# Attention 2's closing: half of the output projection moved ahead of the last score units, and its bias as one bf16 product

## The reference, cut to what matters

```python
def _L1_xattn_ref(x, cond, Wq, bq, Wkv, bkv, Wp, bp):
    ...
    q = _fq_sym(q, axis=-1)
    k = _fq_sym(k, axis=-1)
    v = _fq_sym(v, axis=2)
    attn = jnp.einsum('bhqd,bhkd->bhqk', q, k)
    attn = jax.nn.softmax(attn.astype(jnp.float32), axis=-1)
    attn = _fq_unsigned(attn, axis=-1)
    out = jnp.einsum('bhqk,bhkd->bhqd', attn, v)
    out = jnp.transpose(out, (0, 2, 1, 3)).reshape(B, N, C)
    return out @ Wp + bp
```

## Time and profile before

| what | value |
|---|---|
| time, median of 3 executions | 891.05 us (890.66 to 892.91) |
| the profiled execution's own time | 892.17 us |
| its span, first to last instruction | 890.4 us |
| PE busy | 714.0 us (80%) |
| DVE busy | 534.0 us (60%) |
| ACT busy | 368.7 us (41%) |
| POOL busy | 303.3 us (34%) |
| mean granted TensorE clock | 0.889 |

### The profile page before, as it was taken

The page is one execution under the profiler, slowest core; times in us unless marked ns, Lnnn a source line. Parts: engine busy times, 40 slices in busy tenths (PEclk is TensorE's granted clock), DMA queues, the critical chain, the costliest instruction groups (busy, mean ns, idle before and its releaser), DMA issues.

```text
span 890.4 us, 14503 instructions
## 1 busy us (share of the span) xinstructions
PE 714.0 (80%) x5356; PEld 501.8 (56%) x5356; DVE 534.0 (60%) x1244; ACT 368.7 (41%) x658; POOL 303.3 (34%) x332
## 2 busy tenths in 40 slices
PE   5987798997588788887889980892966579999997
PEld 3445465676355555555657860471444446777776
DVE  3896855667899999996475545827776530000014
ACT  4002022424799999996222323342663122221210
POOL 2941130000277777775007506300320072000024
PEclk9997899997899999897898995796898569999999
DMA  7311174520199999999204848000013132515413
GB/s 239 132 59 48 26 148 159 197 74 1 23 176 193 161 198 169 183 174 161 102 25 118 146 126 279 10 0 1 0 54 137 47 87 91 207 48 182 160 39 118
DMA packets 139133, 100.08 MB, mean 112 GB/s; under 512 B 109204, under 2 KB 125238, under 8 KB 137016
## 3 DMA queue, kind: packets, MB, share of 16 engines
q1 hardware_dynamic: 132552, 81.19, 37.8%
q0 software_dynamic: 6224, 17.96, 7.6%
q10 hardware_dynamic: 288, 0.00, 0.0%
HBM read 61.15 MB, written 10.72 MB: 81 GB/s over the span
## 4 chain that ended last, share of the span: by engine, by line
PE 34%; issue 11%; DVE 10%; POOL 4%; ACT 4%; DMA 3%; POOLq 0%; DVEq 0%; ACTq 0%
PE psum L2342 7%; PE psum L2361 5%; PE psum L1661 3%; PE psum L1938 2%; PE psum L214 2%; ACT both L1332 2%; POOL both L568 2%; PE psum L1676 1%; DVE xnT L1438 1%; PE psum L1242 1%; PE psum L2372 1%; PE psum L1520 1%; DMA both<-both 1%; PE psum L621 1%; PE psum L635 1%
## 5 line engine op out<-in xcount | busy, mean ns | idle before, releaser
L1153 POOL TENSOR_SCALAR both<-both 128x1024 f16<-128x1024 f32 x128 | 133.7, 1045 | 162.8 <-ACT both L1332 155.0
L1438 DVE TENSOR_SCALAR_CACHE_REDUCE xnT<-psum,both 128x1024 bf16<-128x1024 f32 x128 | 157.5, 1278 | 9.1 <-PE psum L1242 8.9
L1332 ACT ACTIVATE both<-psum,both 128x1024 f32<-128x1024 f32 x128 | 153.5, 1210 | 9.2 <-DVE xnT L1438 8.7
L1242 PE MATMUL psum<-both 128*128 128x512 bf16 x256 | 84.4, 415 | 32.2 <-ACT both L1332 28.0
L2342 PE MATMUL psum<-both 128*128 128x320 f32 x256 | 73.5, 441 | 3.8 <-ACT both L556 3.8
L1263 PEld LDWEIGHTS psum<-both 128*128 128x128 f16 x1024 | 63.3, 98 | 22.7 <-DMA both<-both 8.3
L2421 ACT ACTIVATE both<-psum 128x320 f32<-128x320 f32 x64 | 27.6, 437 | 110.0 <-PE psum L2342 92.1
L1263 PE MATMUL psum<-both 128*128 128x16 f16 x1024 | 67.7, 171 | 6.4 <-DMA both<-both 2.8
L1264 PE MATMUL psum<-both,minus_base 128*128 128x16 f16 x1024 | 66.5, 170 | 0.0
L1264 PEld LDWEIGHTS psum<-both,minus_base 128*128 128x128 f16 x1024 | 58.6, 98 | 10.8 <-issue 2.7
L2342 PEld LDWEIGHTS psum<-both 128*128 128x128 f32 x256 | 48.8, 194 | 24.1 <-issue 5.3
(11 more groups left out here) (379 smaller groups left out, 1460.5 us busy)
## 6 DMA issues: line engine op xcount, KB each, us to landing
both<-in_l_experts SPq DMA_DIRECT2D x50, 384.0 KB, 3.7
both<-in_l_experts SPq DMA_DIRECT2D x16, 1024.0 KB, 5.5
grouped_y_dram<-both SPq DMA_DIRECT2D x31, 128.0 KB
ctok<-in_ctx SPq DMA_DIRECT2D x2, 1024.0 KB, 7.5
both<-kpad_dram SPq DMA_DIRECT2D x1, 2048.0 KB, 8.0
moe_xn_dram<-xn POOLq DMA_DIRECT2D x4, 512.0 KB, 3.9
both<-bp SPq DMA_DIRECT2D x2, 1024.0 KB, 12.1
moe_y_dram<-both POOLq DMA_DIRECT2D x7, 256.0 KB, 3.1
```

The costliest lines, as they stand in the source:

```text
L1153: nc.gpsimd.tensor_scalar(r2[n % RSLOTS2], e2[:, n % ESLOTS2, :], 255.0, HALF_BASE, ALU.mult, ALU.add).then_inc(sem("r2_ready"), 1)
L1242: last = nc.tensor.matmul(bank[2 * (n % SRING2) + half], qz2[:, h % 2, h // 2, t * P:(t + 1) * P], kT2[:, h // 2, half * 512:(half + 1) * ...
L1332: nc.scalar.activation(e2[:, n % ESLOTS2, :], scores_at(n), ACT.Exp, bias=bias2[:, n:n + 1], scale=s2[:, t * H2 + h:t * H2 + h + 1], accum ...
L1438: nc.vector.tensor_scalar(scaled2[n % 2], scores_at(n), ns2[:, t * H2 + h:t * H2 + h + 1], None, ALU.mult, ALU.min, accum_out=bias2[:, n:n ...
```

## The change

The projection's contraction is split at its middle. Its first half (the first 8 heads) is turned, copied and multiplied behind the last score unit, between the last `values`; the second half alone is left behind the last `scale_out`. The bias becomes one bf16 product a tile: `three_rows` (1 in rows 0 to 2) times `bp2_rows`, whose three rows are the bias split in three bf16 parts. The accumulators move to banks 0 to 3, the turned blocks to banks 4 and 5. The copies of the turned blocks are shared: bank 4 to DVE (`out_turned`), bank 5 to ACT. Three constants are made ahead: the bias is loaded into three rows, POOL makes `three_rows`, and DVE makes `bp2_rows` with eight small instructions behind `shared0.vector`.

```diff
@@ -699,6 +699,8 @@
         onesf = sb("onesf", [P, P])
         first_row = sb("first_row", [P, P])
         bp2 = sb("bp2", [P, D])
+        bp2_rows = sb("bp2_rows", [P, D], BF16)
+        three_rows = sb("three_rows", [P, P], BF16)
         bv4 = sb("bv4", [P, D])
         before = sb("before", [P, P], BF16)
         rw0 = sb("rw0", [P, DC, 32])
@@ -979,6 +981,7 @@
             seq.step(nc.vector.scalar_tensor_tensor(moe0.weight, moe0.weight, 2.5, bcast(wsum, 2, E0), ALU.mult, ALU.mult))
             moe0.slots_vector(dve, seq, bank[5], lambda: shared0.up_vector(dve, 1))
             shared0.vector(dve, seq, 2)
+            bias_rows2_vector(dve, seq)
             dve.wait_ge(sem("vf2_ready"), 4)
             seq.step(nc.vector.tensor_reduce(sv2[:], vT2, AX.X, ALU.max, apply_absolute_value=True))
             keys_begin_vector(dve, seq)
@@ -1126,7 +1129,7 @@
                              (bqk2[:, 0, :], A["l1_bq"].rearrange("(o n) -> o n", o=1).to_broadcast([P, D])),
                              (bqk2[:, 1, :], A["l1_bkv"][0:D].rearrange("(o n) -> o n", o=1).to_broadcast([P, D])),
                              (bv2[:], A["l1_bv"]),
-                             (bp2[0:1, :], A["l1_bp"].rearrange("(o n) -> o n", o=1))):
+                             (bp2[0:3, :], A["l1_bp"].rearrange("(o n) -> o n", o=1).to_broadcast([3, D]))):
                 sp.dma_start(dst, src).then_inc(sem("l1x_loaded"), 16)
 
         L1X_LOADS = 16 * 7
@@ -1139,6 +1142,8 @@
                                     pattern=[[-1, P]], channel_multiplier=1).then_inc(sem("small_consts"), 1)
             nc.gpsimd.iota(block_no[:], pattern=[[1, NB3]], base=0, channel_multiplier=0,
                            allow_small_or_imprecise_dtypes=True).then_inc(sem("small_consts"), 1)
+            nc.gpsimd.affine_select(out=three_rows[:], in_=onesb[:], compare_op=ALU.is_ge, fill=0.0, base=2,
+                                    pattern=[[0, P]], channel_multiplier=-1).then_inc(sem("small_consts"), 1)
 
         def l1x_rounds_gpsimd(pool):
             for n in range(H2 * NT):
@@ -1266,6 +1271,20 @@
 
             U = H2 * NT
             pe.wait_ge(sem("small_consts"), 15)
+            def turn_out(c):
+                for half in range(2):
+                    for t in range(4):
+                        last = nc.tensor.transpose(bank[4 + half][:, t * P:(t + 1) * P], o2[:, 4 * half + t, c * P:(c + 1) * P], ident[:])
+                    last.then_inc(sem("oT2_blocks"), 1)
+
+            def project_out(c, t):
+                ps = bank[t // 2][:, t % 2 * D:(t % 2 + 1) * D]
+                if c == 0:
+                    nc.tensor.matmul(ps, three_rows[:], bp2_rows[:], start=(t % 2 == 0), stop=False, skip_group_check=True)
+                last = nc.tensor.matmul(ps, oT2[:, c, t * P:(t + 1) * P], wp2[:, c, :], start=False, stop=(c == 1), skip_group_check=True)
+                if c and t % 2:
+                    last.then_inc(sem("proj2_done"), 1)
+
             for n in range(U + LAG2):
                 if n < U:
                     scores(n)
@@ -1273,17 +1292,23 @@
                     turn(n - TURN_LAG2)
                 if n >= LAG2:
                     values(n - LAG2)
+                if n == U:
+                    pe.wait_ge(sem("o2_ready"), 2)
+                    pe.wait_ge(sem("e2_ready"), U - 2)
+                    turn_out(0)
+                if n >= U + LAG2 - 4:
+                    if n == U + LAG2 - 4:
+                        pe.wait_ge(sem("oT2_ready"), 2)
+                        pe.wait_ge(sem("e2_ready"), U)
+                        pe.wait_ge(sem("small_consts"), 17)
+                    t = 2 * (n - (U + LAG2 - 4))
+                    project_out(0, t)
+                    project_out(0, t + 1)
             pe.wait_ge(sem("o2_ready"), H2 // GH2)
-            pe.wait_ge(sem("small_consts"), 6)
-            transpose_T(pe, o2, sem("oT2_blocks"))
+            turn_out(1)
             pe.wait_ge(sem("oT2_ready"), 4)
             for t in range(NT):
-                ps = bank[4 + t // 2][:, t % 2 * D:(t % 2 + 1) * D]
-                nc.tensor.matmul(ps, first_row[:], bp2[:], start=True, stop=False)
-                for c in range(DC):
-                    last = nc.tensor.matmul(ps, oT2[:, c, t * P:(t + 1) * P], wp2[:, c, :], start=False, stop=(c == DC - 1))
-                if t % 2:
-                    last.then_inc(sem("proj2_done"), 1)
+                project_out(1, t)
 
         def l1x_values_scalar(act):
 
@@ -1345,11 +1370,9 @@
                 if n >= COPY_LAG2 and turned_by_tensor(n - COPY_LAG2) and not copied_by_vector(n - COPY_LAG2):
                     copy_T(n - COPY_LAG2)
 
-            for half in range(2):
-                for c in range(DC):
-                    act.wait_ge(sem("oT2_blocks"), 2 * half + c + 1)
-                    nc.scalar.activation(oT2[:, c, half * 512:(half + 1) * 512], bank[2 * half + c], ACT.Copy,
-                                         scale=sv2[:, c:c + 1]).then_inc(sem("oT2_ready"), 1)
+            for c in range(DC):
+                act.wait_ge(sem("oT2_blocks"), 2 * c + 2)
+                nc.scalar.activation(oT2[:, c, 512:T], bank[5], ACT.Copy, scale=sv2[:, c:c + 1]).then_inc(sem("oT2_ready"), 1)
 
         def values_steps(dve, seq):
 
@@ -1386,6 +1409,15 @@
 
         def round2(src, dst):
             return nc.vector.tensor_scalar(dst, src, MAGIC, MAGIC, ALU.add, ALU.subtract)
+
+        def bias_rows2_vector(dve, seq):
+
+            dve.wait_ge(sem("l1x_loaded"), L1X_LOADS)
+            seq.mark(split3(seq, lambda i: y0_parts[:, 0, i], y0_left[:, 0], bp2[:]))
+            seq.wait()
+            seq.step(nc.vector.tensor_scalar(bp2_rows[:], y0_parts[:, 0, 0], ident[:, 0:1], None, ALU.mult))
+            for k in range(1, 3):
+                seq.step(nc.vector.scalar_tensor_tensor(bp2_rows[:], y0_parts[:, 0, k], ident[:, k:k + 1], bp2_rows[:], ALU.mult, ALU.add))
 
         def keys_begin_vector(dve, seq):
             take2(dve, seq, 1, kf2, 4, 0)
@@ -1479,9 +1511,15 @@
             for n in range(U - VCOPY_LAG2, U):
                 if copied_by_vector(n):
                     copy_T(n)
+            def out_turned(c):
+                dve.wait_ge(sem("oT2_blocks"), 2 * c + 1)
+                nc.vector.tensor_scalar(oT2[:, c, 0:512], bank[4], sv2[:, c:c + 1], None, ALU.mult).then_inc(sem("oT2_ready"), 1)
+
+            out_turned(0)
             sums_times(H2 // GH2 - 1)
             sums_turned(H2 // GH2 - 1)
             scale_out(H2 // GH2 - 1)
+            out_turned(1)
             for b in range(4):
                 if b:
                     seq.wait()
@@ -1491,7 +1529,7 @@
                 if b == 3:
                     ln_finish(dve, seq, 3, 0)
                 dve.wait_ge(sem("proj2_done"), b + 1)
-                seq.mark(nc.vector.scalar_tensor_tensor(x[:, 2 * b:2 * b + 2, :].rearrange("p a d -> p (a d)"), bank[4 + b],
+                seq.mark(nc.vector.scalar_tensor_tensor(x[:, 2 * b:2 * b + 2, :].rearrange("p a d -> p (a d)"), bank[b],
                                                         tg[:, 1:2], x[:, 2 * b:2 * b + 2, :].rearrange("p a d -> p (a d)"),
                                                         ALU.mult, ALU.add))
             seq.wait()
```

## The result

| | kernel before | changed kernel |
|---|---|---|
| median | 892.01 us (887.37 to 896.14, 19 executions) | 895.56 us (891.30 to 901.90, 19 executions) |
| ratio, 95% interval | 1 | 1.0044 [1.0026, 1.0063] |
| the profiled execution's own time | 892.17 us | 894.02 us |
| its span | 890.4 us | 892.0 us |
| mean granted TensorE clock | 0.889 | 0.887 |

The changed kernel is slower by about 3.5 us, outside the forecast range by 0.4 us. Single executions scatter with a standard deviation of 2.6 us, so a mean says more than one time: over all executions of this study the kernel before has a mean of 891.4 (127 of them) and the changed one 895.3 (33), a difference of 4.0 us with a standard error of 0.5.

A forecast was written before the change was run, and what follows sets the result against it. The closing was taken as one unbranched chain, with DVE waiting for PE's products. 2.6 us gained, less 0.4 and 1.65 to 3.1 lost at half clock, gave +0.2 on 892.17: 892.4 us, range 889.0 to 895.2.

The forecast's parts named there:

- Part 1: Preparations: DVE's eight small instructions, 3.4 us at most, fit an idle stretch of 6.91 us; nothing on the path.
- Part 2: Eight turns moved behind unit 121: 1.04 us with drain at full clock, inside PE's idle time; cost nothing.
- Part 3: New wait ahead of the first pair of products: PE waits for DVE's copy of bank 4 until 420.1.
- Part 4: Three pairs of products between the last units: 1.07 us each at full clock, 2.14 at half; unit 127 ends 5.2 later.
- Part 5: Behind the last scaling: first add at 430.0, 1.2 us earlier; with DVE's waits gone, third add 2.6 us earlier.
- Part 6: Norm: PE idles 3.9 us, clock falls to half; turns lose 0.4 us, the up-projection 1.65 to 3.1.
- Rival (a): Clock doesn't fall in the norm, or returns at once, so the 2.6 us gain stays: 889.6 us; chance 0.16.
- rival (b): Clock stays full through the closing too, first add at 428.6, gain 4.0 us: 888.2 us; chance 0.12.
- Rival (c): Products ahead of the last values at half clock throughout, decided when the third pair begins: 895.2 us; chance 0.22.
- +0.2: Predicted net change in us, the middle of -0.55 and +0.9: the closing's gain is given back in the norm.

The follow-up runs named there:

- e3_prep: Kernel before with only the preparations added (bias in three rows, constants made ahead), unread by the old closing: 892.19 us, ratio 1.0007.
- b_look1: Kernel before, unchanged, run again for one more trace; the two such single executions took 888.25 and 887.90 us.
- e4_copy: Changed kernel with DVE's copy of the first turned block put ahead of its copies of the last units: 891.97 us, 0.9999 to the kernel before.
- a_again: Changed kernel, unchanged, run again for a second trace and more times: 894.69 us, 1.0035 to the kernel before.
- e1_fill: Changed kernel with eight unread f32 products on PE in the idle stretch ahead of the norm's turns: 889.91 us, 0.9985 to the kernel before.
- e2_bias: Kernel before with the preparations and the bf16 bias product in the old place, contraction not split: 888.96 us, ratio 0.9962.
- e8_all: Changed kernel with the earlier copy, eight unread products ahead of the norm's turns and three ahead of the down-projection: 887.00 us, 0.9957 to the kernel before.
- e5_copy_fill: Changed kernel with the earlier DVE copy and eight unread products ahead of the norm's turns: 886.26 us, 0.9951 to the kernel before.

## Why the prediction was wrong

**What held.** Part 1: the eight instructions fill 116.48 to 119.9 and leave 3.46 us idle in the changed kernel; e3_prep shows no cost of them either. Part 2: the moved turns cost 1.07 us at full clock in free time. Part 3: PE waits for DVE's copy, till 419.36 (predicted 420.1; the copy of unit 127 itself came 0.8 earlier). Part 4: the bias product, which no row of before showed, takes 0.12 us at full clock and 0.21 to 0.23 at half, as taken (0.11). The last scaling ends at 426.93 (predicted 427.1). Part 5: the first add at 430.06 (predicted 430.0), the third at 433.63 without a wait for PE. The chain of waits of the changed kernel (start, duration, what) shows the pairs, slow and then fast:

```profile
419.36 0.40 PE psum L1283
419.76 0.85 PE psum L1284 x2
...
422.09 0.23 PE psum L1283
422.32 0.85 PE psum L1284 x2
...
424.65 0.12 PE psum L1283
424.77 0.43 PE psum L1284 x2
```

Part 6: 3.72 us idle (predicted 3.9), the clock at 0.50 behind it, the up-projection between five and seven. So the mechanism was the forecast one. Rival (a) and rival (b) did not come: the clock fell in the norm, and also at 417.7, just behind PE's wait of 1.77 us for POOL. Rival (c) gave 895.2, close to what was measured, but it isn't what happened: its point of decision was a half clock at the third pair, and the third pair began at 424.65 at full clock, 0.1 us behind the clock's return. The time fits (c), the trace doesn't.

**The Trainium skill** (TensorE: Matmul & The Clock Gate, Part 4: PE-mode transpose) says that transposes don't bring TensorE to full rate. b_look1 again speaks otherwise: from 420.73 until the clock's return at 424.1 PE made nothing but its sixteen turns. They don't do it each time: in the trace the same turns ran from 421.88, and the clock came back only at 430.0.

**The step that failed is the base of the sum,** the closing that the +0.2 ("what is won in the closing is given back in the norm") was added to. Parts 5 and 6 compare with a closing in which the products ran at half clock until 430.0. On that base the terms come out nearly as predicted: counted from the last row maximum, the third add is 23.42 - 21.08 = 2.34 us earlier (predicted 2.6), and from there to the router it takes 16.62 instead of 13.34, 3.28 more (predicted 2.8, between 2.05 and 3.5): +0.9 instead of +0.2. But three of four traces of the kernel before have the short closing (with e3_prep, whose closing is the old one too, three of five). Against that one the third add is only 0.4 to 0.7 us earlier, and the same 3.3 are paid: 37.65 (the changed kernel's mean) less 34.96 is +2.7. Over the four traces of before the closing costs 37.65 - 35.41 = +2.2 us; with e3_prep's as a fifth, +1.9. The prediction saw that its execution lay 1.1 us above the median and wrote that three times can't say which of them shows this closing. It then kept the sum on the long one and put the doubt into the range alone. Of the 3.8 us between the forecast +0.2 and the +4.0 of the means, this base is 1.3 (36.76 against 35.41), the largest part that is found inside the closing; the sizes of Parts 5 and 6 are 0.7; 1.8 lie outside the closing. By luck the time itself was missed by less: the 892.17 that the sum starts from is 0.8 above the mean of the kernel before.

**The size of Part 6** was a smaller error. The turns lost 0.56 instead of 0.4, the up-projection 2.84 where the middle of 1.65 and 3.1 was taken. The longer of the two stretches of the trace, where the gap was of this kind, would have been the better neighbour.

**What the prediction did not price** is Part 3's pause. It let the pairs start at 420.1, where unit 126 had begun at 420.00, and put no price on the wait itself. e4_copy shows 2.9 us, mostly because the clock comes back 3.4 us earlier without the pause. That is no part of the error, since the first add came where the sum had it; it is a gain that the change left lying.

**What stays open.** The closing explains about +2.2 of the +4.0. In the four traces each, what follows the router takes 2.4 us longer in the changed kernel, though in a_again it is 0.6 shorter (440.09) than in the trace (440.68). About 0.9 of the 2.4 has been lost by the end of the expert blocks (their last product starts 80.2 to 80.6 us behind the router, against 79.0 to 80.1), but e3_prep, whose closing is the old one, has 80.3 there too. The 2.4, and what comes ahead of the closing (1.3 us shorter in the changed kernel's four), are smaller than the spread of one kernel's traces there (4.7 and 8.3 us), and no run places them. One hint: the mean of e1_fill's executions, 890.5, is 4.9 us below the changed kernel's, with a standard error of 0.9, while its closing is only 3.2 shorter; so a part of what is lost further on may hang on the norm's clock as well. That isn't shown. Nor is it settled why the old closing has two forms: the clock falls 1.6 to 1.8 us behind the last row maximum in the short one and at 3.4 and 4.3 in the long ones, and comes back at 11.9 to 12.0 and at 17.0 and 18.0; what decides between them wasn't tried.

## What to carry to other kernels

Moving products away from the last stretch of a stage also moves them away from the engine that needs them to stay fast: price the hole they leave at the half clock of the work behind it, and try a few unread products in the hole before giving the change up (here 895.6 became 889.9, and 886.3 with the wait removed). Read a stage from several traces before a sum is made on it, above all where a clock step lies inside it. A forecast that names the right number can still have the wrong rival: compare the rival's point of decision, not its time.

## What the runs showed of the hardware

In the first trace of the changed kernel the clock fell inside a gap of 3.72 us on TensorE and stayed at half for 10.2 us (22.2 to 32.4 us behind the last row maximum), and that cost 3.4 us on the path (0.56 in the turns, 2.84 in the up-projection); in e2_bias two gaps of about 1 us with 1.41 us of turns between them were followed by 3.4 us at half clock. A single pause of 1.03 us, ahead of products while the clock was at half, put the clock's return off to 11.9; without the pause it was at 8.5, in e4_copy and in e8_all. In the changed kernel these moments repeat: its four traces have the fall at 5.1 or 5.2 and the return at 11.9 or 12.0, and the second fall at 22.1 to 22.3 in three and 25.5 in one, with the same return at 32.4 or 32.5. The kernel before lands on one of two forms 2 us apart, and e5_copy_fill and e8_all, with the same edits up to the router, differ by 1.3 us.
